# Both layer norms' normalisation by ScalarE instead of VectorE, with a bias made by GpSimd

## The reference, cut to what matters

```python
h = _layernorm(x, axis=-1) * (1 + ca) + sa          # first norm
x = x + ga * attention(h)                            # 16 heads, causal, rotary
h = _layernorm(x, axis=-1) * (1 + cb) + sb
x = x + gb * ffn(h)
# ffn begins with a norm of its own:
xn = (h - mu) * rsqrt(var + 1e-05) * ln_scale + ln_bias
x_attn = xn @ attn_w.T + attn_b + h                  # then 8 experts, fixed slices of tokens
```

## Time and profile before

| | |
|---|---|
| median of 3 runs | 2080.36 us (2070.25 to 2081.01) |
| the profiled execution | 2082.45 us, of which the span from first to last instruction is 2080.7 |
| busy share of the span | PE 91%, DVE 82%, ACT 65%, POOL 11% |
| busy in project | PE 102.42, DVE 105.55, ACT 54.48, POOL 74.76 of 141.60 us |
| busy in mix | PE 95.78, DVE 105.97, ACT 33.09, POOL 67.56 of 137.60 us |
| idle of PE in mix for DVE's xn | 28.1 us in 7 waits, the longest 7.3 |
| granted PE clock | 0.94 in project, 0.84 in mix, 0.941 over the span |

### The profile page before, as it was taken

The page is one execution under the profiler, slowest core; times in us unless marked ns, Lnnn a source line. Parts: engine busy times, 40 slices in busy tenths (PEclk is TensorE's granted clock), DMA queues, the critical chain, the costliest instruction groups (busy, mean ns, idle before and its releaser), DMA issues. The chain is left out here.

```text
span 2080.7 us, 36982 instructions
## 1 busy us (share of the span) xinstructions
PE 1893.3 (91%) x13224; PEld 961.4 (46%) x13224; DVE 1711.1 (82%) x2969; ACT 1347.8 (65%) x2675; POOL 237.4 (11%) x187
## 2 busy tenths in 40 slices
PE   7841989999999999999999999999999996869998
PEld 4530534334444443444444344444434325638887
DVE  5961789989989999999899999989998604977886
ACT  3410456676687787778678787777887893226553
POOL 4720000000000000000000000000000002544442
PEclk9975789999999999999899999999999998979999
DMA  5866000000002000000300000010000004102331
GB/s 174 228 173 129 17 10 9 9 1 9 10 2 79 17 10 9 10 10 3 71 24 9 9 10 3 10 32 9 2 1 2 2 1 153 54 23 98 103 111 40
DMA packets 58716, 87.11 MB, mean 42 GB/s; under 512 B 9428, under 2 KB 31444, under 8 KB 58552
## 3 DMA queue, kind: packets, MB, share of 16 engines
q1 hardware_dynamic: 58552, 84.89, 14.4%
HBM read 58.19 MB, written 20.97 MB: 38 GB/s over the span
## 5 line engine op out<-in xcount | busy, mean ns | idle before, releaser
L942 DVE TENSOR_REDUCE mx<-banks 128x1 f32<-128x512 f32 (+3 forms) x2304 | 1313.5, 637 | 174.2 <-PE banks L843 136.5
L910 ACT ACTIVATE prob<-banks 128x512 f32<-128x512 f32 (+3 forms) x2304 | 1117.2, 605 | 353.1 <-PE banks L819 232.0
L881 PE MATMUL banks<-prob,v_all 128*17 128x512 f32 (+3 forms) x4608 | 580.8, 577 | 0.0
L843 PE MATMUL banks<-k_aug,q_aug 48*128 48x512 f32 (+3 forms) x2304 | 520.6, 446 | 59.7 <-POOL later_h L980 27.9
L819 PE MATMUL banks<-q_aug,k_aug 52*128 52x512 f32 (+3 forms) x2304 | 524.9, 452 | 51.5 <-issue 32.7
L819 PEld LDWEIGHTS banks<-q_aug,k_aug 52*128 52x128 f32 x2304 | 229.4, 190 | 441.8 <-ACT prob L910 289.2
L843 PEld LDWEIGHTS banks<-k_aug,q_aug 48*128 48x128 f32 x2304 | 234.4, 192 | 314.7 <-ACT prob L910 203.6
L987 POOL CAST nm_p<-nm 128x16 fp32r<-128x16 f32 x32 | 6.8, 214 | 1483.7 <-DVE nm L948 1483.7
L881 PEld LDWEIGHTS banks<-prob,v_all 128*17 128x17 f32 x4608 | 76.9, 95 | 158.6 <-ACT prob L910 82.1
L851 PEld LDWEIGHTS banks<-id_h,later_h 64*128 64x128 f32 x1024 | 97.8, 200 | 3.1
L851 PE MATMUL banks<-id_h,later_h 64*128 64x128 f32 x1024 | 97.2, 264 | 0.0
(11 more groups left out here) (115 smaller groups left out, 1509.5 us busy)
## 6 DMA issues: line engine op xcount, KB each, us to landing
parts_scratch<-p SPq DMA_DIRECT2D x64, 256.0 KB, 4.2
w_s<-in_w SPq DMA_DIRECT2D x16, 1024.0 KB, 5.3
xs<-in_x SPq DMA_DIRECT2D x16, 512.0 KB, 4.5
k_aug<-parts_scratch SPq DMA_DIRECT2D x64, 128.0 KB, 3.2
q_aug<-parts_scratch SPq DMA_DIRECT2D x64, 128.0 KB, 2.5
cs<-in_rope SPq DMA_DIRECT2D x8, 512.0 KB, 5.9
k_aug<-parts_scratch SPq DMA_DIRECT2D x64, 64.0 KB, 2.9
q_aug<-parts_scratch SPq DMA_DIRECT2D x64, 64.0 KB, 2.5
```

The lines of the kernel that those rows point to most:

```text
L843: mm = nc.tensor.matmul(bank(banks[r])[:, 0:width], q_aug[rows, n % QRING, b, t * P:(t + 1) * P], k_aug[rows, b, key_slot(n, kc)[0], 0:wid ...
L881: mm = nc.tensor.matmul(pv[32 * j:32 * j + VW, q0:CW], v_all[:, g, kb, j, :], prob[:, s % PROBS, j, q0:CW], start=(kb == 0), stop=(s == LA ...
L910: nc.scalar.activation(prob[:, s % PROBS, j, q0:CW], bank(from_bank)[:, q0:CW], ACT.Exp, scale=float(HD) ** -0.5).then_inc(act_read, 1)
L942: nc.vector.tensor_reduce(mx[:, n % QRING, r, b, t, kc:kc + 1], bank(from_bank)[:, 0:unit_width(i)], AX_X, ALU.max).then_inc(dve_read, 1)
```

## The change

DVE's two `normalise` functions go. ACT gets them: one activation per tile, `Identity(x * scale + bias)`, with the inverse standard deviation as a per-partition scale and a new `shift` as bias. POOL makes `shift` as minus the mean times the inverse standard deviation, with two more small instructions per chunk and norm (128 by 4 elements). In ACT's slot of project the normalisation stands first; in mix it stands last but for the weights' high parts. DVE's aggregates also wait for the `shift` of two chunks before, which still reads the tile that they write.

```diff
@@ project, POOL: inverse_std
                 nc.gpsimd.tensor_scalar(var_e[:, off % 2, :], mv[:, off % 2, :, 1], EPS, None, ALU.add)\
                     .then_inc(var_done, 1)
+                nc.gpsimd.tensor_scalar(mean_n[:, off % 2, :], mv[:, off % 2, :, 0], -1.0, None, ALU.mult)\
+                    .then_inc(mean_done, 1)
                 pool.wait_ge(var_done, i * 2 + off + 1)
                 nc.gpsimd.tensor_tensor(rstd[:, off % 2, :], var_e[:, off % 2, :], half_neg[:, :], ALU.pow)\
                     .then_inc(rstd_done, 1)
+                pool.wait_ge(mean_done, i * 2 + off + 1)
+                pool.wait_ge(rstd_done, i * 2 + off + 1)
+                alone(pool, passed_pool)
+                nc.gpsimd.tensor_tensor(shift[:, off % 2, :], mean_n[:, off % 2, :], rstd[:, off % 2, :], ALU.mult)\
+                    .then_inc(shift_done, 1)
@@ project, DVE: moments, before the first aggregate
+                    if off >= 2 and t == 0:
+                        dve.wait_ge(shift_done, i * 2 + off - 1)
@@ project, DVE: slot (and normalise(0, 0) ahead of the slots)
-                if off + 1 < CHUNKS:
-                    normalise(i, off + 1)
@@ project, ACT
+            def normalise(i, off):
+                par = off % 2
+                act.wait_ge(shift_done, i * 2 + off + 1)
+                if off:
+                    act.wait_ge(hT_ps, HALF * (i * 2 + off))
+                for t in range(TILES):
+                    nc.scalar.activation(xn[:, t, :], xs[:, par, t, :], ACT.Identity, bias=shift[:, par, t:t + 1],
+                                         scale=rstd[:, par, t:t + 1]).then_inc(xn_done, 1)
+
+            normalise(0, 0)
             act.wait_ge(mod_ev, 2)
             def slot(i, off):
+                if off + 1 < CHUNKS:
+                    normalise(i, off + 1)
                 if off:
                     part1(i, off - 1)
@@ mix, POOL: inverse_std gets the same two instructions for both norms
@@ mix, ACT: slot, behind h2T
+                if there(i, off):
+                    if off >= 2:
+                        act.wait_ge(scaled, i * 2 + off - 1)
+                    normalise(0, i, off, lambda t: x1[:, bass.ds((i * 2 + off) * TILES + t, 1), :]
+                              .rearrange("p o d -> p (o d)"))
+                if there(i, off - 1):
+                    if off >= 2:
+                        act.wait_ge(x3_ps, FREE + HALF * (i * 2 + off - 2))
+                    normalise(1, i, off - 1, lambda t: h2[:, (off - 1) % 2, t, :])
@@ mix, DVE: slot, behind both moments
-                if there(i, off):
-                    if off >= 2:
-                        dve.wait_ge(scaled, i * 2 + off - 1)
-                    normalise(0, i, off, tile)
-                if there(i, off - 1):
-                    if off >= 2:
-                        dve.wait_ge(x3_ps, FREE + HALF * (i * 2 + off - 2))
-                    normalise(1, i, off - 1, lambda t: h2[:, last, t, :])
```

More of the change, by code:

```diff
@@ L327, in project_block @@
     rstd = sb("rstd", [P, 2, TILES])
+    mean_n = sb("mean_n", [P, 2, TILES])
+    shift = sb("shift", [P, 2, TILES])
     xn = sb("xn", [P, TILES, D])
@@ L345, in project_block @@
                                                       sem("rstd_done"), sem("xn_done"))
+    mean_done, shift_done = sem("mean_done"), sem("shift_done")
     hT_ps, hT_ev = sem("hT_ps"), sem("hT_ev")
@@ L554, in _ @@
             moments(0, 0)
-            normalise(0, 0)
             dve.wait_ge(mod_ps, 1)
@@ L1034, in mix_block @@
     rstd = sb("rstd2", [P, 2, 2, TILES])
+    mean_n = sb("mean_n2", [P, 2, 2, TILES])
+    shift = sb("shift2", [P, 2, 2, TILES])
     xn = sb("xn2", [P, 2, 2, TILES, D])
@@ L1045, in mix_block @@
         [sem(f"m_{name}{k}") for k in range(2)] for name in ("st_done", "mv_done", "var_done", "rstd_done", "xn_done"))
+    mean_done, shift_done = ([sem(f"m_{name}{k}") for k in range(2)] for name in ("mean_done", "shift_done"))
     scaled, h2_done = sem("m_scaled"), sem("h2_done")
@@ L1159, in _, with normalise @@
         def _(act):
-            begin(act, x3T_ev)
+            begin(act, x3T_ev, xn_done[1])
+            def normalise(k, i, off, src):
+                par = off % 2
+                act.wait_ge(shift_done[k], i * 2 + off + 1)
+                for t in range(TILES):
+                    nc.scalar.activation(xn[:, k, par, t, :], src(t), ACT.Identity, bias=shift[:, k, par, t:t + 1],
+                                         scale=rstd[:, k, par, t:t + 1]).then_inc(xn_done[k], 1)
             def take_o(i, off):
@@ L1202, in _ @@
         def _(dve):
-            begin(dve, x1_done, xa_done, xn_done[1])
+            begin(dve, x1_done, xa_done)
             dve.wait_ge(w_in, 48)
@@ L1212, in moments @@
                     dve.wait_ge(st_done[k], TILES * (i * 2 + off) + t + 1)
+                    if t == 0 and off >= 2:
+                        dve.wait_ge(shift_done[k], i * 2 + off - 1)
                     alone(dve, passed_dve)
                     nc.vector.bn_aggr(mv[:, k, par, t, :], stats[:, k, par, t, :]).then_inc(mv_done[k], 1)
[L1216 to L1221, removed]
             def slot(i, off):
@@ L1272, in inverse_std @@
                     .then_inc(var_done[k], 1)
+                nc.gpsimd.tensor_scalar(mean_n[:, k, par, :], mv[:, k, par, :, 0], -1.0, None, ALU.mult)\
+                    .then_inc(mean_done[k], 1)
                 pool.wait_ge(var_done[k], i * 2 + off + 1)
@@ L1275, in inverse_std @@
                     .then_inc(rstd_done[k], 1)
+                pool.wait_ge(mean_done[k], i * 2 + off + 1)
+                pool.wait_ge(rstd_done[k], i * 2 + off + 1)
+                alone(pool, passed_pool)
+                nc.gpsimd.tensor_tensor(shift[:, k, par, :], mean_n[:, k, par, :], rstd[:, k, par, :], ALU.mult)\
+                    .then_inc(shift_done[k], 1)
             def slot(i, off):
```

## The result

The changed kernel takes **2067.21 us** (median of 20 runs, 2058.39 to 2075.74), the kernel before 2075.32 (median of 20 runs, 2065.48 to 2083.65): a ratio of 0.996 with the 95% interval 0.9945 to 0.9974. So it is 8.1 us faster, 0.4%, where 3 were forecast, and stays within the 0.5% that the prediction called the same.

The account below looks back on a forecast made before the run. No engine was full; rings of waits bound project (DVE, ACT, POOL) and mix (PE waiting 28.1 us for DVE's xn). Project +20 and mix -23 gave -3: 2079.5 profiled, 2077.4 us as median, range 2064 to 2089.

Parts of the forecast that it names:

- The very first normalise 0.5 later: Project's start: two more small instructions and hand-overs delay the first normalise, and PE's first turn and all behind it, by 0.5.
- Rival 1: POOL's extra instructions don't queue behind DVE: project +13.7, mix -25, total -11, 2069 us; chance 0.15.
- the lower bound: Project +13.7: mean_n slips past cut, shift follows rotate's first half, part1 2.0 late per slot; first slot +3.2.
- Rival 2: ACT's normalise is hidden in project as well, which costs only +0.5 there: 2058 us; chance 0.05.
- Rival 3: The lower PE clock takes project over: up to 27, project total +24, 2104 us; chance 0.06.
- Rival 4: Mix's ring isn't freed, normalise 1 ends after Wo: mix -12, total +8, 2088 us; chance 0.1.
- Rival 5: Each of the 24 normalises costs what ACT needs more than DVE (1.9 against 1.4): +12, 2092 us; chance 0.04.
- some 3 us of slower turns go: Mix: PE's turns take 1.96 after a wait, 1.09 without; three or four times 0.87 go with the waits.
- a bound (-28): Mix's far bound, if the end gets faster too: its L1151 took 6.00 where another took 3.70.
- the link's lateness: Mix's start: each chunk's link is 1.1 longer, 0.5 on POOL and 0.6 on ACT.
- the waits that were to return: Mix, 8.4 of 28.1: first xn 1.3, h2 1.9, chunk 6's xn 3.0, last h2 1.7, last xn 0.5.
- 0.8 to spare: Middle of mix: POOL finishes h2 at 8.4 in the slot and PE turns it at 9.2.

Follow-up runs that it names:

- e2: Project as changed, mix as in the kernel before: 2094.1 us, ratio 1.0116 to the kernel before.
- e4: The whole change, but project's mean_n made by DVE behind its aggregates instead of by POOL: 2062.23 us, ratio 0.9942 to the kernel before.
- e3: The whole change, but project's normalise on ACT stands between the two q,k copies, not ahead of part1: 2045.15 us, ratio 0.9868 to the kernel before.
- e5: Kernel before with only mix's normalise of h2 on ACT, that of x1 on DVE; POOL makes both shifts: 2046.48 us, ratio 0.9873.
- e1: Mix as changed, project as in the kernel before: 2050.0 us, ratio 0.9894 to the kernel before.
- e6: Kernel before with only mix's normalise of x1 on ACT, that of h2 on DVE; POOL makes both shifts: 2060.1 us (one run).

## Why the prediction was right, and where it wasn't

**Project: right, step by step but for the start.** Forecast +20, measured +19.84, and +19.7 in e2. The slot: 16.4 forecast, 16.38 measured. The first slot 4.3 longer: from by_cos of chunk 0 to that of chunk 1 it is 15.68, where it was 11.23 (25.41 to 36.64), 4.45. The very first normalise 0.5 later: it starts at 9.54 against 9.02, and PE's first q,k product at 18.80 against 18.22. But by_cos of chunk 0 starts at 25.38 against 25.41, so this 0.5 did not reach the slots. It is less than the start's scatter: in the four kernels that leave project alone that by_cos comes at 24.24 to 25.85, their slots agree to 0.02, and their projects end at 140.50 to 142.13. Four activations, 1.9 until part1: 1.98 (588 ns each), from a pointer scale and bias priced at the difference of two evictions and added to the spacing of two short copies. Shift at 2.4 behind rotate's start: 68.57 - 66.29 = 2.3.

**Rival 1 and the lower bound rested on a step that is wrong in five slots of six.** Both had shift get in behind rotate's first half if POOL's queue were one instruction shorter. In e4 it was, the power ended as that bound said, and shift still ended with the second half. In the first slot the bound (3.2 longer) came: 14.34 - 11.23 = 3.1. POOL's small instruction was let in only when the DVE instruction beside it had ended. The Trainium skill, SBUF — State Buffer, "SBUF: two separate sides", states this as a lock: of a DVE instruction with two SBUF inputs and a GpSimd one that reads SBUF, whichever starts first has the shared ports for its whole length. E4's 1.27 against 0.20 agrees, and the cost so comes in steps of a DVE instruction.

Two things the traces don't bear out. Who starts first in the trace does not settle it within 0.01 us: in e4 rotate's second half, 0.006 ahead of shift, went through, but in mix of the kernel before a normalise that starts 0.009 ahead of POOL's second h2 instruction (1784.90) was held until that ended. And POOL's power does not hold DVE off for its whole length: in the changed kernel its last 0.9 us lie beside rotate's second half, and the two halves still take 2.35.

**Rival 2 (hidden in project) is wrong for this place and right for another**: e3. The prediction saw ACT's idle 5.56 and that it is over before shift exists; it did not look for the place a few us further on, ahead of the second q,k copy, where the same 2 us cost nothing. **Rival 3** did not come: PE's clock in project fell from 0.94 to 0.90 and its busy time rose from 102.42 to 110.00, but ACT and POOL set the slot. **Rival 4** did not come: slots are 10.2, 10.4 forecast.

**Rival 5, the page's rule,** would have cost the 24 normalises 12 us. The Trainium skill, ScalarE: Activation LUTs, "Rules for kernel authors", gives add and multiply to VectorE, with a figure for bf16; the tiles here are f32. For x1 in mix the runs don't speak against it (e5's mix is 2.2 shorter than e1's); for h2, beside POOL, e6's mix is 17.6 longer than with ACT. The rule counts an engine's time per element and not what runs beside it.

**Mix: the mechanism right, the size 3.7 short** (-23 against -26.7). The mis-sized term is "some 3 us of slower turns go". PE's busy time in mix fell by 95.78 - 87.16 = 8.6 for the same 384 matmuls, at a granted clock of 0.91 against 0.84 (1.00 is the level of 2.4 GHz, 0.50 that of 1.2). The turns of xn and the products with attn_w, first before, then after (count; busy us, mean ns; idle before them):

```profile
L1107 PE MATMUL banks<-id_f,xn 128*128 128x128 f32 x64 | 12.9, 366 | 28.1 <-DVE xn L1220 28.1
L1151 PE MATMUL banks<-x3T,w_a 128*128 128x512 f32 x64 | 32.1, 649 | 1.3 <-issue 1.3
```

```profile
L1123 PE MATMUL banks<-id_f,xn 128*128 128x128 f32 x64 | 8.4, 274 | 2.9 <-ACT xn L1182 2.8
L1167 PE MATMUL banks<-x3T,w_a 128*128 128x512 f32 x64 | 29.6, 606 | 1.3 <-issue 1.2
```

The turns of xn fell by 4.5, those of the attention's output, three of which had been slow behind a late xn, by 2.4 (11.6 to 9.2), and those of h2 rose by 0.5 (10.0 to 10.5): 6.4 where 3 were forecast. The products with attn_w fell by 2.5, nearly all of it in the last one: 3.67 at a granted clock of 1.00, behind waits of 1.8 and 1.2, where it had been 6.00 at 0.61, behind a wait of 6.43 ahead of its turn and one of 0.92. The prediction had that as a bound (-28) and not in the sum. Wo took 33.4 in both kernels. PE's waits, all causes together, fell from 41.9 to 23.4, by 18.5, where 28.1 - 8.4 = 19.7 was forecast; with the busy time that is 27.1, beside the block's 26.7.

The two are not independent, as the first h2 shows: PE's Wo ahead of it took 3.69 at a granted clock of 1.00 where it had taken 6.62 at 0.55, so PE came to that turn 3.05 sooner and waited for it 4.17 longer (6.27 against 2.10); h2 itself was late by the other 1.1, the link's lateness as forecast. The Wo behind that wait then took 5.15 at 0.70, where it had taken 3.62.

Of the waits that were to return, the first xn was not late (1.3 forecast), chunk 6's by 2.79 (3.0), the last h2 by 1.77 (1.7), the last xn by 0.1 (0.5). In the middle POOL's h2 was to have 0.8 to spare; instead PE waited for it 0.2 to 0.9 in each of six slots, some 3 us together. The reason given why DVE and POOL would no longer exclude each other, that DVE keeps no instruction with two SBUF tiles there, is not the whole of it: the normalise reads one tile and two pointer scalars and had been held up all the same.

One step of the end was wrong by little. POOL's low parts were to end while PE's last product runs. POOL and DVE at the block's end:

```profile
1843.62 4.66 POOL L1331 TENSOR_TENSOR w_lo<-w_s,w_hi 128x1024 fp32r<-128x1024 f32 x2
```

```profile
1847.29 0.75 DVE L1272 SCALAR_TENSOR_TENSOR att_o<-banks,ab_col,h2T 128x512 f32<-128x512 f32 x1 [0.89 <-PE banks L1167]
```

They end at 1848.28, 1.0 after PE (1847.25) and 0.24 after DVE's last addition (1848.04): with the block that much shorter they are what ends last in it.

**The sum.** The forecast lies 10.2 above the median after. Half of that is the change (-8.1 for -3): 3.7 from mix and 1.0 from experts, where the block's first 20 matmuls took 7.3 us at a granted clock of 0.61 before and 6.3 at 0.73 after. The other half is the start: the three runs shown before had a median of 2080.36, twenty have 2075.32. The time measured lies 3.2 inside the range's lower end. What sets attend's length in one execution stays open; PE's busy time and clock go with it: 1489.93 of 1585.80 us at 0.94 before, 1480.68 of 1576.20 at 0.95 after, 1475.27 of 1572.20 at 0.96 in e1. So it is for whole runs: of the twenty after, the fastest had a mean granted clock of 0.953, the slowest 0.943.

## What to carry to other kernels

Work moved to an engine with room is free or not by its place in that engine's order, not by the room: find the instruction that the ring waits for, and put what waits for a late input behind it (13.26 or 16.38 a slot for the same work). Take from VectorE what is held up beside GpSimd's two-input work, and leave there what isn't: moving one of mix's two normalises gave all of the gain, and moving the other as well gave nothing more. When waits of TensorE go, read its busy time at both clocks as well: faster matmuls were 8.6 of the 27.1 us here. And a matmul that gets faster ahead of a late input comes back as wait there.

## What the runs showed of the hardware

- A GpSimd add or multiply on 128x4 took 0.20 to 0.35 us with no DVE instruction of two SBUF inputs beside it, and 1.05 to 1.27 with one. Starting within 0.1 us of the end of one such instruction it took 0.20 with none behind, and 1.27, until the next one's end, where another followed (both in e4).
- GpSimd's power on 128x4 took 1.04 us by itself; behind a two-input DVE instruction it ended 0.9 after that one's end, and these 0.9 us did not lengthen the next (1.21).
- VectorE's one-input normalise with two pointer scalars took 0.41 us, also beside GpSimd's power, and 2.35 to 2.50 beside a GpSimd instruction with two inputs on 128x1024 (before, e6). Its bn_stats of four 128x256 tiles took 1.40 us, no longer than without, though the first three lay beside such an instruction (at 1783.64 in the changed kernel, with GpSimd's h2 from 1782.16 to 1784.52).
- ScalarE's 128x256 activation took 588 ns with a pointer scale and a pointer bias, four 2.07; with the scale alone four took 1.71.
- Unchanged code of attend took 1571.6 to 1585.8 us over nine profiled executions, 0.9%, where the change studied here is worth 0.4%.
